# The tail of a linear-attention layer: x added by another engine, the router's matmul made wider and the base matmul narrower, one norm taken by statistics, and two tiles of norm work interleaved

## The reference

```python
x = layernorm(x + attention(x))      # 32 heads of 128, gated, with an RMS norm over the 4096 head outputs
x = layernorm(x + ffn(x))

# ffn
base_out = x @ base_W.T + base_b                       # 512 -> 512
probs = softmax(x @ router_W.T + router_b)             # 15 routes
top 8 routes, mapped to 8 experts -> w[token, expert]
h = x @ A.T                                            # 8 experts x rank 16 = 128 columns
out = base_out + (h * w) @ B.T * 2.0
```

## Time and profile before

| | |
|---|---|
| median of 3 runs | 1020.52 us (1020.47 to 1022.36) |
| the profiled execution, own time | 1021.64 us |
| span of the profiled execution | 1019.9 us |
| mean granted TensorE clock | 0.997 |
| busy: TensorE, VectorE, ScalarE, GpSimd | 1003.3, 775.8, 668.4, 357.5 us |
| instructions | 15716 |

### The profile page before, as it was taken

The page is one execution under the profiler, slowest core; times in us unless marked ns, Lnnn a source line. Parts: engine busy times, 40 slices in busy tenths (PEclk is TensorE's granted clock), DMA queues, the critical chain, the costliest instruction groups (busy, mean ns, idle before and its releaser), DMA issues.

```text
span 1019.9 us, 15716 instructions
## 1 busy us (share of the span) xinstructions
PE 1003.3 (98%) x5620; PEld 873.7 (86%) x5620; DVE 775.8 (76%) x1092; ACT 668.4 (66%) x1116; POOL 357.5 (35%) x336
## 2 busy tenths in 40 slices
PE   9999999999999999999999999999999999999996
PEld 7878988889888898889888898888988898888785
DVE  6777975787867977778757978679777788699754
ACT  6577754787477763777547874777637775576635
POOL 1453232441443223532324414432225323322662
PEclk9999999999999999999999999999999999999998
DMA  6011111110211111111211102111111112012302
GB/s 201 29 60 52 48 58 52 47 47 28 68 42 47 51 64 44 46 52 47 62 48 48 47 29 66 42 47 55 60 47 42 52 48 68 21 48 72 107 2 82
DMA packets 48813, 55.44 MB, mean 54 GB/s; under 512 B 4320, under 2 KB 40032, under 8 KB 48736
## 3 DMA queue, kind: packets, MB, share of 16 engines
q1 hardware_dynamic: 48736, 54.44, 16.8%
HBM read 52.33 MB, written 2.10 MB: 53 GB/s over the span
## 4 chain that ended last, share of the span: by engine, by line
PE 88%; DVE 4%; POOL 3%; ACT 2%; issue 2%; DMA 1%; SPq 0%; POOLq 0%; ACTq 0%; DVEq 0%
PE ps L1810 19%; PE ps L1811 19%; PE ps L1812 19%; PE ps L1804 9%; PE ps L1805 8%; PE ps L1806 8%; PE ps L1917 1%; PE ps L1902 1%; PE ps L1919 1%; PE ps L1904 1%; POOL rstd L1689 1%; DVE yl L1032 1%; POOL acc L1695 1%; DVE s L1032 1%; DVE wl L1051 1%
## 5 line engine op out<-in xcount | busy, mean ns | idle before, releaser
L1810 PE MATMUL ps<-xh,wh 128*128 128x512 f32 x658 | 261.9, 398 | 0.7 <-ACT stg L426 0.6
L1811 PE MATMUL ps<-xl,wh 128*128 128x512 f32 x658 | 257.2, 391 | 0.0
L1812 PE MATMUL ps<-xh,wl 128*128 128x512 f32 x658 | 256.2, 389 | 0.0
L1710 POOL TENSOR_TENSOR stage<-stage 128x512 f32<-128x512 f32 x61 | 87.8, 1440 | 329.8 <-DMA stage<-stream 329.6
L1730 POOL TENSOR_TENSOR sqacc<-sqacc,sq 128x512 f32<-128x512 f32 x64 | 92.3, 1442 | 272.4 <-ACT sq L537 272.4
L1032 DVE TENSOR_TENSOR wl<-stage,wh 128x1024 fp32r<-128x1024 f32 (+2 forms) x145 | 158.7, 1104 | 32.3 <-ACT wh L378 32.2
L378 ACT ACTIVATE wh<-stage 128x1024 fp32r<-128x1024 f32 (+2 forms) x145 | 122.0, 854 | 53.1 <-PE ps L1806 33.8
L1812 PEld LDWEIGHTS ps<-xh,wl 128*128 128x128 f32 x658 | 123.5, 188 | 26.7
L1810 PEld LDWEIGHTS ps<-xh,wh 128*128 128x128 f32 x658 | 123.5, 188 | 24.3 <-issue 1.0
L1811 PEld LDWEIGHTS ps<-xl,wh 128*128 128x128 f32 x658 | 123.8, 188 | 22.1
L1810 PE MATMUL ps<-wh,xh 128*128 128x256 f32 x392 | 112.8, 288 | 0.0
(11 more groups left out here) (189 smaller groups left out, 2268.7 us busy)
## 6 DMA issues: line engine op xcount, KB each, us to landing
stage<-stream SPq DMA_DIRECT2D x61, 384.0 KB, 3.3
stage<-stream SPq DMA_DIRECT2D x42, 256.0 KB, 2.8
stage<-stream SPq DMA_DIRECT2D x63, 128.0 KB, 2.1
dec<-decay SPq DMA_DIRECT2D x32, 128.0 KB, 2.0
acc<-xt SPq DMA_DIRECT2D x8, 256.0 KB, 5.9
v<-x SPq DMA_DIRECT2D x8, 256.0 KB, 5.1
out<-acc SPq DMA_DIRECT2D x8, 256.0 KB, 2.0
sfull<-lora_router SPq DMA_DIRECT2D x1, 288.0 KB, 4.7
```

Of the source, the lines that this page charges most:

```text
L1710: nc.gpsimd.tensor_tensor(stage[:, s, 1:5:3, :], stage[:, s, 0:6:5, :], stage[:, s, 7:8, :].broadcast_to([P, 2, U]), ALU.add).then_inc(t_p ...
L1810: nc.tensor.matmul(dst, wt[0], mv_[0], start=start, stop=False, skip_group_check=True)
L1811: nc.tensor.matmul(dst, wt[0], mv_[1], start=False, stop=False, skip_group_check=True)
L1812: return nc.tensor.matmul(dst, wt[1], mv_[0], start=False, stop=stop, skip_group_check=True)
```

## The change

It has four parts, all of them in the tail.

- x is added by VectorE: `scale_acc` on ScalarE and `add_x` on GpSimd go, for tiles 3 to 7, and one VectorE instruction a tile comes in their place (`scaled`, `acc * rms + x`).
- The router's matmuls are widened by base columns. `XB = 256 - 144 = 112` columns of `base_W` are appended to `lora_router`, so `router_and_lora` has matmuls of 256 columns, its transfer is 512 KB, and the splits of `ar` are 1024 elements wide. `base` works on the other 400 columns (its first matmul of a tile is still 512 wide and writes zeros to the 112). VectorE adds the 112 columns to `acc` (`first_columns`), two tiles at a time.
- The last tile's second norm is done by statistics: an addition without row sum, `bn_stats`, `bn_aggr`, two GpSimd instructions (eps and power), and one VectorE instruction that subtracts the mean and multiplies.
- The norm steps are written in another order: GpSimd takes minus the mean together with `centre` (`means`), ahead of the wait for the variance, and the `means` of tile t + 1 stand before `affine(t)`; ScalarE takes the variance of tile t + 1 before it normalizes tile t. The low parts of the base weights (`tail_rows_lo`), the split of B, and `lora_transposed(0)` on TensorE have new places.

```diff
+AW = 256
+XB = AW - AR
...
+            def scaled(t):
+                dve.wait_ge(rms_done, 1)
+                dve.wait_ge(o_added, (GROUPS - 1) * TT)
+                dve.wait_ge(res_in[t], 16)
+                nc.vector.scalar_tensor_tensor(out=acc[:, t, :], in0=acc[:, t, :], scalar=rms[:, t:t + 1],
+                                               in1=res[:, t, :], op0=ALU.mult, op1=ALU.add).then_inc(acc_scaled, 1)
...
+            def first_columns(f):
+                dve.wait_ge(bias_added, HG * f + HG)
+                for b in range(2):
+                    t = HG * f + 2 * b
+                    nc.vector.tensor_tensor(acc[:, t:t + 2, 0:XB], acc[:, t:t + 2, 0:XB], hl_bank(f, b)[:, :, AR:AW],
+                                            ALU.add).then_inc(columns_added, 1)
...
             def second_residual(t):
                 dve.wait_ge(ffn_done, t + 1)
                 dve.wait_ge(bias_added, t + 1)
+                dve.wait_ge(columns_added, t // 2 + 1)
+                if t == TT - 1:
+                    nc.vector.tensor_tensor(acc[:, t, :], acc[:, t, :], ps[:, FFN_BANK[t], :], ALU.add)\
+                        .then_inc(ffn_read, 1)
+                    return
...
```

ScalarE's order:

```diff
-            for t in range(3, 6):
-                scale_acc(t)
             tail_rows_hi(6)
             variance(0)
-            scale_acc(6)
+            variance(1)
+            normalize(0, ln1_done)
+            variance(2)
+            normalize(1, ln1_done)
+            tail_rows_hi(7)
+            transposed(0)
+            variance(3)
+            normalize(2, ln1_done)
             nc.scalar.activation(arh, ar, ACT.Copy).then_inc(ar_hi, 1)
-            scale_acc(7)
...
             variance(4)
             normalize(3, ln1_done)
+            transposed(1)
+            normalize(4, ln1_done)
             transposed(2)
-            normalize(4, ln1_done)
             variance(5)
-            lora_weights_hi()
+            normalize(5, ln1_done)
+            transposed(3)
+            transposed(4)
             variance(6)
...
             transposed(7)
+            lora_weights_hi()
             lora_transposed(0)
...
-            normalize(TT + 4, out_ready)
-            variance(TT + 7)
-            for t in range(5, TT):
+            for t in range(4, 7):
                 normalize(TT + t, out_ready)
```

VectorE's and GpSimd's order, and TensorE's functions:

```diff
             first_residual(2)
+            scaled(3)
             first_residual(3)
+            scaled(4)
             first_residual(4)
             transposed(0)
-            tail_rows_lo(4)
-            tail_rows_lo(5)
             minus(arl, ar, arh).then_inc(ar_lo, 1)
+            scaled(5)
+            first_residual(5)
             transposed(1)
-            first_residual(5)
-            tail_rows_lo(6)
+            tail_rows_lo(4)
+            scaled(6)
             transposed(2)
             first_residual(6)
+            tail_rows_lo(5)
+            scaled(7)
+            transposed(3)
+            first_residual(7)
+            tail_rows_lo(6)
             tail_rows_lo(7)
...
             router_weights(0)
+            first_columns(0)
+            minus(bch_l, ..., bch_h).then_inc(t_lo, 2)
...
+            second_residual(TT - 1)
+            dve.wait_ge(ffn_read, TT)
+            link(nc.vector.bn_stats(stat[:, :], acc[:, TT - 1, :]))
+            nc.vector.bn_aggr(mv[:, :], stat[:, :]).then_inc(last_stats, 1)
+            dve.wait_ge(last_rstd, 1)
+            nc.vector.tensor_scalar(acc[:, TT - 1, :], acc[:, TT - 1, :], mv[:, 0:1], rstd[:, 2 * TT - 1:2 * TT],
+                                    ALU.subtract, ALU.mult).then_inc(last_ready, 1)
...
+            means(0)
+            for t in range(4):
+                means(t + 1)
+                affine(t)
             affine(4)
+            for t in range(5, TT):
+                means(t)
+                affine(t)
+            for t in range(TT):
                 add_bias(t)
-            for n, m in ((8, 2), (10, 2), (12, 2), (14, 1), (15, 1)):
+            for n, m in ((8, 2), (10, 2), (12, 2), (14, 1)):
+                means(n, m)
                 affine(n, m)
+            pool.wait_ge(last_stats, 1)
+            link(nc.gpsimd.tensor_scalar(mv[:, 1:2], mv[:, 1:2], EPS, None, ALU.add))
+            nc.gpsimd.tensor_tensor(rstd[:, 2 * TT - 1:2 * TT], mv[:, 1:2], half_power[:, 0:1], ALU.pow)\
+                .then_inc(last_rstd, 1)
...
             base(2)
             router_and_lora(1)
+            lora_transposed(0)
             base(3)
-            lora_transposed(0)
             base(4)
```

More of the change, by code:

```diff
@@ L1646, in _ @@
             router_weights(0)
+            first_columns(0)
+            dve.wait_ge(t_hi, 2 * NLOADS)
+            minus(bch_l, stage[:, (TAIL_LOAD + 4) % 2, 0:2, :].rearrange("p a n -> p (a n)"), bch_h).then_inc(t_lo, 2)
             router_logits(1)
@@ L1650, in _ @@
             router_weights(1)
+            first_columns(1)
             second_residual(0)
@@ L1659, in _ @@
             second_centre(3)
-            for t in range(4, TT):
+            for t in range(4, TT - 1):
                 second_residual(t)
@@ L1675, in link, with means @@
                 pool.wait_ge(pool_step, steps[0])
[L1677 to L1681, removed]
+            def means(n, m=1):
+                tiles = slice(n, n + m)
+                if n < TT:
+                    pool.wait_ge(x1_done, n + m)
+                    nc.gpsimd.tensor_scalar(centre[:, tiles], total[:, tiles], -1.0 / HID ** 1.5, None, ALU.mult)\
+                        .then_inc(mean_done, 1)
+                else:
+                    pool.wait_ge(ffn_read, n - TT + m)
+                nc.gpsimd.tensor_scalar(neg_mean[:, tiles], total[:, tiles], -1.0 / HID, None, ALU.mult)
             def affine(n, m=1):
@@ L2199, in router_and_lora, with mm3_first @@
                 last.then_inc(hl_done, 1)
+            def mm3_first(bank, wt, hi, lo):
+                nc.tensor.matmul(ps[:, bank, :], wt[0], hi, start=True, stop=False, skip_group_check=True)
+                nc.tensor.matmul(ps[:, bank, XB:W], wt[0], lo[:, XB:W], start=False, stop=False, skip_group_check=True)
+                nc.tensor.matmul(ps[:, bank, XB:W], wt[1], hi[:, XB:W], start=False, stop=False, skip_group_check=True)
             def base(t):
@@ L2214, in base @@
                     row = TAIL_BASE + 2 * k
-                    mm3(ps[:, FFN_BANK[t], :], (xh[:, k, tile(t)], xl[:, k, tile(t)]),
-                        (wh[:, row:row + 2, :], wl[:, row:row + 2, :]), k == 0, False)
+                    hi, lo = [w[:, row:row + 2, :].rearrange("p a n -> p (a n)") for w in (wh, wl)]
+                    if k == 0:
+                        mm3_first(FFN_BANK[t], (xh[:, k, tile(t)], xl[:, k, tile(t)]), hi, lo)
+                    else:
+                        mm3_onto(ps[:, FFN_BANK[t], XB:W], (xh[:, k, tile(t)], xl[:, k, tile(t)]), (hi[:, XB:W], lo[:, XB:W]),
+                                 False, False)
             def lora(t):
-                mm3(ps[:, FFN_BANK[t], :], (qh[:, tile(t)], ql[:, tile(t)]), (bch_h, bch_l),
+                if t == 0:
+                    pe.wait_ge(t_lo, 2 * NLOADS)
+                mm3_onto(ps[:, FFN_BANK[t], :], (qh[:, tile(t)], ql[:, tile(t)]), (bch_h, bch_l),
                     False, True).then_inc(ffn_done, 1)
@@ L2331 @@
     blocks.append(rows(wo[HEADS - 2], wo[HEADS - 1]))
-    blocks.append(rows(wb[0], wb[1]))
-    blocks.append(rows(wb[2], wb[3]))
+    rest = wb.copy()
+    rest[:, :, :XB] = 0
+    blocks.append(rows(rest[0], rest[1]))
+    blocks.append(rows(rest[2], rest[3]))
     blocks.append(rows(wB, np.zeros_like(wB)))
     xt = x.reshape(2, W, 2, 2, P).transpose(0, 2, 4, 3, 1).reshape(4, P, 2 * W)
-    lora_router = np.zeros((P, KT, AR), np.float32)
+    lora_router = np.zeros((P, KT, AW), np.float32)
+    lora_router[:, :, AR:] = wb[:, :, :XB].transpose(1, 0, 2)
     lora_router[:, :, :NEXP * RANK] = np.asarray(L0_ffn_A).reshape(NEXP * RANK, KT, P).transpose(2, 1, 0)
```

80 lines of the change are left out of this document (21 added, 59 removed).

## The result

| | before | changed |
|---|---|---|
| median, us | 1020.92 (1020.47 to 1022.36, 4 runs) | 1015.54 (1014.85 to 1015.99, 4 runs) |
| ratio of the runs, 95% interval | | 0.9944 [0.9927, 0.9961] |
| span of the profiled execution | 1019.9 | 1014.2 |
| its own time | 1021.64 | 1015.99 |

The change is 5.4 us faster by the medians. The forecast was 1014.7 us, 5.8 us faster, in a range of 1012.0 to 1017.8.

The account below looks back on a forecast made before the run. TensorE first waits for norms, then is the bound; ScalarE and GpSimd set the end. -4.3 us up to lora_transposed(1) and -1.45 at the end give -5.8, so 1014.7 us median, range 1012.0 to 1017.8.

Parts of the forecast that it names:

- The sum: Whole tail: -4.3 us up to lora_transposed(1) and -1.45 us at the end, together -5.8 us.
- TensorE's own work: Tail matmuls: router 0.1185 us each, 0.34 us more per half; base 0.18 us at 400 columns, 0.52 us less per tile.
- Rival 3: Base matmuls: 400 columns take as long as 512, six tiles lose 3.1 us, 1017.8 us; chance 0.08.
- rival 4: VectorE's queue behind the split of ar: ScalarE's copy comes late and the change is slower, 1022.5 us; chance 0.03.
- The first norm: TensorE's waits ahead of the transposes: 1.30 of 2.70 us remain, so the first router half ends 1.06 us earlier.
- rival 2: First norm: all waits ahead of the transposes go, fewer collisions and early low part of tile 2, 1013.4 us; chance 0.17.
- rival 1: First norm gives nothing: scaled and the longer ar split hold up GpSimd, the 2.70 us waits stay, 1016.6 us; chance 0.23.
- The middle: First router half to lora_transposed(1): base saves 1.55 us twice, a 0.52 us wait goes, router costs 0.34; lora_transposed(1) at 997.8.
- The worth of the columns: Moving 112 base columns into the router matmuls: six base tiles save 3.1 us, each wider router half costs 0.34 us.
- The end: From B (start of lora_transposed(1)) to the end: GpSimd's queue sets the last tile, ready 1015.9 instead of 1017.35, -1.45 us.

Follow-up runs that it names:

- e8: The kernel before with x of tiles 3 to 7 added by VectorE and nothing else changed: median 1018.46 us, ratio to before 0.9986.
- e1: The changed kernel with the base columns back in base (router matmuls 144 columns wide, base 512, no first_columns): median 1017.15 us, ratio to before 0.9962.
- e2: The changed kernel, its order kept, with x of tiles 3 to 7 scaled by ScalarE and added by GpSimd again: median 1020.44 us.
- e4: The changed kernel with GpSimd's eight bias additions replaced by one-column instructions, so base_b is missing from the result: median 1014.62 us.
- e10: The changed kernel with GpSimd's last four bias additions held back until router_weights(0) is done: median 1014.27 us, ratio to before 0.9938.
- e5: The changed kernel with lora_transposed(0) behind base(3) again and its splits behind the second half's exponent and top-8: median 1015.85 us.
- e3: The changed kernel with the last tile's second norm by row sum, ScalarE's variance and ScalarE's normalization as before: median 1016.78 us.
- e6: The changed kernel with the second norm of tiles 2 and 3 applied by VectorE, not ScalarE: median 1015.12 us, ratio to before 0.9944.

## Why the prediction was right, step by step

**The sum.** The tail is 5.21 us shorter where 5.8 was forecast. The span is 5.7 us shorter, because this execution also came to the tail 0.49 us earlier, with the same code. By the medians it is 5.4. That the sum came so near is in part luck: up to `lora_transposed(1)` two misses stand against each other, 0.42 us more from the first norm and a wait of 1.05 us that the sum does not have.

**TensorE's own work.** Right, with small misses: 0.1215 us for a router matmul (forecast 0.1185) and 0.183 for 400 columns (forecast 0.18). A `base` tile takes 2.34 us (973.50 to 975.84) where it took 2.86, minus 0.52 as forecast. Rival 3 is out. So is rival 4: its sign, a late copy of `ar`, is not there (the split starts at 961.58).

**The first norm.** The forecast had the first router half 1.06 us earlier; it is 1.48 (30.28 - 28.80). `transposed(0)` does not wait, where 0.45 us was expected: one collision, not two, fell on tile 0's chain, that of GpSimd's power, which takes 0.57 us alone:

```profile
954.00 0.88 POOL L1725 TENSOR_TENSOR rstd<-var,half_power 128x1 f32<-128x1 f32 x1
```

That is the first half of rival 2; the second, an early low part of tile 2, did not come. The wait ahead of `transposed(4)` for VectorE's low part was forecast with 0.85 us and is 0.79. Which part of the change is at work there the runs tell: x on VectorE takes away all of the 2.70 us (e8), with the narrow split the interleaved order adds nothing to it (e1 against e8), and the 0.79 us comes from the 1024-wide split (e1). The order would have cost time with x on GpSimd (e2).

The Trainium skill, SBUF — State Buffer, section "Who interferes with whom", has two VectorE inputs in SBUF and a GpSimd read exclude each other for the whole instruction. The traces agree (1.80 us in e2 against 0.75, 1.22 us in the changed kernel against 0.22 in e4). Yet rival 1, which I drew from it, did not come true. The collisions with `scaled` are there, GpSimd's power taking 0.94 us at 956.12 and 0.93 us at 962.96, but they fall on tiles 1 and 4, whose normalized tiles are ready at 958.19 and 965.02, ahead of the 959.34 and 966.15 at which TensorE is free for them. And what the rule counts against `scaled` (0.75 us each) it counts more heavily against the 1.3 us additions that `scaled` replaces.

**The middle.** Here a step failed. The sum for `lora_transposed(1)` has no term for a wait ahead of `lora_transposed(0)`, which the change moves ahead of `base(3)`; the forecast walks VectorE's weighting for the second half only. With its times there would have been none: the low part of tile 7 at 981.5, the 5.0 us that `router_weights(0)` took before (985.16 to 990.16) and 0.7 for `first_columns` give 987.2, against TensorE at 982.1 + 48 x 0.1185 = 987.8. But `router_weights(0)` took 6.7 us (980.77 to 987.47), and `lora_transposed(0)` waited 1.05 us. The bias additions do "start at about 975, as they did before", as the forecast says, but VectorE comes to its first compare 4.39 us earlier and the additions end only 1.84 us earlier (984.23 against 986.07). Before, one instruction of the weighting lay under them, now three:

```profile
977.31 8.76 POOL L1701 TENSOR_TENSOR acc<-acc,sq 128x512 f32<-128x512 f32 x7
```

```profile
985.16 0.98 DVE L1568 TENSOR_TENSOR above<-prob,top 128x60 f32<-128x60 f32 x1
986.18 0.22 DVE L1569 TENSOR_TENSOR equal<-prob,top 128x60 f32<-128x60 f32 x1
```

e4 and e10 show it: without the additions, or with four of them later, the tail is 1.19 and 1.12 us shorter. e5 shows the other side: with `lora_transposed(0)` behind `base(3)` again 0.62 us of it comes back, so its new place is a loss as long as the weighting is held up. With the wait `lora_transposed(1)` came 3.74 us earlier instead of 4.3. The second router half did start without a wait, as forecast. For the second half's weighting the forecast has 996.4; its own terms give 987.8 + 10.3 - 2.95 + 0.7 = 995.9, and 996.39 was measured, 1.55 ahead of TensorE.

**The worth of the columns** was put at 3.1 - 0.68 us, and e1 says 0.9. The parts: 6 tiles of 0.52 us, minus 0.86 for two router halves (5.83 against 5.40 each), minus the 0.79 ahead of `transposed(4)`, minus 0.54 that the wait ahead of `lora_transposed(0)` is longer than in e1 (1.05 against 0.51). 3.1 - 0.86 - 0.79 - 0.54 = 0.91.

**The end.** Forecast -1.45 us from B to the end, measured -1.47 (17.73 to 16.26); the forecast's own terms (1014.2 + 0.9 + 0.7) give 1015.8 for the last tile and not 1015.9, so -1.55. e3 gives 0.84 of it to the last norm. The rest, 0.63, stands in e3 already. Counted from B in both timelines, 0.30 us of it is gained ahead of the third normalization, which no longer waits for `shift`, and 0.23 ahead of the variance of tile 6, which before stood behind TensorE's last tile; no run takes these apart. That GpSimd's queue and not `bn_aggr` would be what the last tile waits for came out as forecast (3.57 us). Behind it stands ScalarE's chain: GpSimd itself waits 2.74 us for ScalarE's variances at 1007.24, and e6, which makes that chain shorter, gains 1.63 us. An order of GpSimd's queue with the last tile first was not run; since ScalarE ends 0.59 us before VectorE, it could give no more than that.

## What to carry to other kernels

When a change makes one engine earlier, look at what the others do in the same microseconds: transfers and fillers that stayed where they were (here the bias additions) come to lie on other instructions, and cost 1.1 us of a 5.2 us gain until half of them are held back. When two parts of a change may act on the same wait, undo each by itself: here one of them takes it all away alone, and the other added nothing to it. And where the scatter of runs is as large as the effect, mark off the changed stretch in the profiles and compare its length, next to the medians and not in their place.

## What the runs showed of the hardware

- A 60-element scan or compare with two SBUF inputs on VectorE took 1.03 and 1.22 us while GpSimd's 128x512 additions (1.26 us each) ran, 0.28 and 0.22 without them (e4). A 512-wide one took 1.80 against 0.75 (e2): the 1.0 us more is as large for the small instruction as for the wide one.
- At a granted clock of 1.00, matmuls of 144, 256, 400 and 512 columns with new weights each follow each other in 0.1115, 0.12, 0.183 and 0.227 us: from 256 columns up it is close to a line (0.42 ns a column), below it almost flat.
- The part ahead of the tail, with the same instructions in all 14 kernels, took 942.6 to 946.4 us; the tail's own marks, where the code up to them is the same, repeat to 0.03 us.
- VectorE's subtract-and-multiply of 128x512 with two column operands took 0.55 us, `bn_stats` of the same size 0.69.
